# Delta-rule layers: v copied to SBUF by ScalarE, multiplied by beta on GpSimd, k and q projected to exchanged banks

## The chip, the cores and the metric

The kernel runs on one core of a Trainium2 chip. A core has five engines with queues of their own: TensorE (PE in the rows, PEld its weight loads), VectorE (DVE), ScalarE (ACT), GpSimd (POOL) and SyncE (SP), which only issues DMAs here. They work on SBUF, 128 partitions wide, and on PSUM, in which matmuls leave their results; GpSimd doesn't take part in reading PSUM here. Engines wait for each other through semaphores. The metric is the device time of one execution in microseconds, and lower is better.

## What is computed

Five stages in a row on x of 16 x 256 x 128: a convolutional token mixer, external attention with a Mamba layer, a mixture of experts, an attention block with two delta-rule ("fast weight") layers, and a second mixture of experts. The change touches the two delta-rule layers alone. The sequence is 254 long by then, there are 16 batches (B), 8 heads (H) and D = 64:

```python
def delta_rule(q, k, v, beta):
    def step(W, inp):
        qt, kt, vt, bt = inp
        wk = jnp.einsum('bhde,bhe->bhd', W, kt)
        v_new = bt * (vt - wk)
        W = W + jnp.einsum('bhd,bhe->bhde', v_new, kt)
        out = jnp.einsum('bhde,bhe->bhd', W, qt)
        return (W, out)
    ...
def fast_ff(x, ln_g, ln_b, slow_w, out_w):
    h = layer_norm(x, ln_g, ln_b)
    qkvb = jnp.einsum('sbi,oi->sbo', h, slow_w).reshape(slen, bsz, H, 3 * D + 1)
    q, k, v, beta = jnp.split(qkvb, [D, 2 * D, 3 * D], axis=-1)
    q = jax.nn.softmax(q, axis=-1)
    k = jax.nn.softmax(k, axis=-1)
    beta = jax.nn.sigmoid(beta)
    attn = delta_rule(q, k, v, beta)
    o = jnp.einsum('sbd,od->sbo', attn.reshape(slen, bsz, H * D), out_w)
    return x + o
```

## The kernel before

`fast_weights` (L1433) computes one such layer and is called twice. The recurrence over 254 tokens is cut into two chunks of 127 per batch, called lanes here (u = 0 and 1). Within a chunk it becomes a triangular system: A holds the products of beta*k with k, the inverse of its unit triangular form is applied to the right-hand side beta*v, and what comes out (`u_new`) gives the state and, with the masked products of q and k (`qk`), the outputs.

A pipeline of stages runs over the batches: `stage(b, ...)` prepares batch b, inverts batch b - 1 and substitutes batch b - 2. Stages 0 and 1 fill it (stage 0 only prepares, stage 1 prepares and inverts), 2 to 15 do all three, 16 and 17 drain it. Each engine walks through the same stages with an order of its own that is written out by hand; semaphores alone tie them. There is no scheduler.

What the engines do in a full stage:

- TensorE: projections of k, beta and q (`project`, L1658; `fw_w`, `fw_xs`), `below_blocks` and `corner_blocks` of the inverse (L1714, L1730), the turns of kb and k (`turn`, L1669), then for each lane the solves and joins (L1746, L1759, L1771), the sum A (`sum_a`, L1682), the projection of v, state, outputs (L1784, L1796, L1811, L1825, L1832), turns of q, the first qk sum (`sum_qk`, L1699), the output projection (L1841) and the second qk sum. Both qk sums of a lane go to two banks, one for even and one for odd heads.
- VectorE: per lane the maximum of k (L2002) and its shift (L2011), then `turn_blocks` (L2053), which turns the 32x32 blocks of the inverse of batch b - 1 that a DMA has brought to `fw_x_rows`; then beta, sums and reciprocals, maximum and shift of q; and between all that the inversion, `go_on` (L2075 product, L2079 subtraction), 31 such pairs in a row, each of which depends on the one before. In between stand `rest(0)` and `rest(1)` (L2044) and the `carried` subtraction (L2119). Behind the inversion come the two right-hand sides (L2037, from PSUM times beta), the mask of the first qk sum (L2059, even heads), the addition of the output projection (L2130) and the mask of the second.
- ScalarE: the exponentials, and nearly all copies out of PSUM, among them the odd heads of qk (L1914).
- GpSimd: kb and k (L1608, L1610), q (L1614), the copy of the next batch to `fw_xs` (L1617), the masks of the odd heads of qk (L1620) and the unit start of the next inversion (L1626).
- SyncE: when the last step of the inversion is done, it writes `fw_lane_x` to DRAM (L1568, two DMAs), reads the next A (L1573), reads the inverse back as rows (L1581, four DMAs, which the turn L2053 waits for) and to `fw_x_t` (L1585).

The banks of PSUM are shared between uses, and a use waits until the last one is read. k is projected to banks 4 and 5, where the qk sums of lane 1 lay, q to 7 and 3, where those of lane 0 lay. So the k projection of the next stage waits for the last mask of this one. The lane tiles of the inversion and `fw_rhs`, `fw_kb`, `fw_k_rows`, `fw_q_rows` are fp32 in SBUF.

## Time and profile before

| | before |
|---|---|
| time, median of 3 runs | 3078.03 us (3076.59 to 3078.49) |
| profiled execution | 3075.59 us, of which the trace spans 3073.7 us |
| VectorE busy | 2118.2 us, 69% |
| TensorE busy | 2422.8 us, 79% |
| ScalarE busy | 1209.8 us, 39% |
| GpSimd busy | 654.5 us, 21% |

The profile is of one execution. Busy shares are averages over stages with different limits, so a change in one layer is read from that layer: its stretch, its waits, and then one stage of it as a timeline. A wait is put down to what ended last by the trace. Spans on GpSimd are rough. The two layers lie at 1350 to 2016 us and at 2148 to 2811 us of the span.

### The profile page before, as it was taken

Reading aid. Unit: us, or ns where it says so; the run is one execution under the profiler, and the core shown is the slowest. Engines: PE = TensorE matmul, PEld = TensorE weight load, DVE = VectorE, ACT = ScalarE, POOL = GpSimd, SP = SyncE. Lnnn points to the kernel's source line nnn. Section 1 sums busy time; section 2 is a strip of 40 time slices with the busy share of each in tenths; the row PEclk is TensorE's granted clock in tenths of the full one; section 3 lists DMA queues with packets and bytes.
Section 4 is the critical chain, followed back from the end, with each engine's and each line's share of the span. In section 5 each row is a group of like instructions: output and inputs, shape, how many; then the busy total and the mean of one; then the engine's idle time right before and its main releaser. Section 6 shows DMA issues by size and latency. Waiting matters only on the chain. (4 is left out here: it accounts for less than half of the span.)

```text
span 3073.7 us, 43978 instructions
## 1 busy us (share of the span) xinstructions
PE 2422.8 (79%) x16426; PEld 1407.0 (46%) x16426; DVE 2118.2 (69%) x4507; ACT 1209.8 (39%) x1941; POOL 654.5 (21%) x632
## 2 busy tenths in 40 slices
PE   6757777777659999977888888777688888876598
PEld 2232222222234444335666666543466666665343
DVE  2347888888946777748888888612788888883332
ACT  4555444545423222243444444234343443441332
POOL 0004555555500000022222222101322222220000
PEclk9878888888879999988888988778798989986699
DMA  1000000000010000002222222210122222220000
GB/s 34 1 9 1 0 0 0 1 0 1 0 42 0 0 1 0 26 11 42 42 39 40 36 39 42 39 25 1 32 42 43 43 42 43 43 41 12 16 1 27
DMA packets 280817, 65.88 MB, mean 21 GB/s; under 512 B 272968, under 2 KB 274464, under 8 KB 280224
## 3 DMA queue, kind: packets, MB, share of 16 engines
q1 hardware_dynamic: 280608, 63.09, 11.0%
q8 instruction: 132, 2.16, 0.3%
q14 instruction: 77, 0.63, 0.1%
HBM read 44.20 MB, written 18.86 MB: 21 GB/s over the span
## 5 line engine op out<-in xcount | busy, mean ns | idle before, releaser
L907 POOL TENSOR_TENSOR ma_hc<-ma_state,ma_c 128x508 f32<-128x508 f32 x256 | 302.1, 1183 | 370.9 <-DVE ma_state L994 186.2
L2079 DVE TENSOR_TENSOR fw_lane_x<-fw_lane_x,fw_lane_p 128x126 f32<-128x126 f32 (+22 forms) x992 | 330.6, 333 | 34.0
L994 DVE TENSOR_TENSOR_SCAN ma_state<-ma_da,ma_ps_dbx 128x510 f32<-128x510 f32 x256 | 311.5, 1217 | 32.6 <-issue 24.1
L2075 DVE TENSOR_TENSOR fw_lane_p<-fw_lane_a,fw_lane_x 128x126 f32<-128x126 f32 (+22 forms) x992 | 273.5, 276 | 29.6
L1658 PE MATMUL fw_p<-fw_w,fw_xs 128*127 128x512 f32 (+1 forms) x512 | 238.2, 600 | 54.0 <-DVE fw_qk L2059 26.3
L809 PE MATMUL ma_ps_y<-ma_hc,const 128*128 128x508 f32 x480 | 257.1, 662 | 8.4 <-POOL ma_hc L907 8.4
L989 DVE TENSOR_TENSOR ma_ps_dbx<-ma_ps_b,ma_dtx 128x508 f32<-128x508 f32 x256 | 172.8, 675 | 39.6 <-PE ma_ps_b L793 39.1
L1094 ACT ACTIVATE ex_sig<-ex_gate,ex_gate_scaled 128x508 f32<-128x508 f32 x128 | 87.5, 683 | 271.2 <-PE ex_gate L1064 271.2
L886 ACT ACTIVATE ma_da<-ma_dt,ma_a 128x508 f32<-128x508 f32 x256 | 168.6, 708 | 39.3 <-DVE ma_dt L946 39.2
L793 PE MATMUL ma_ps_b<-ma_bc,select 128*128 128x508 bf16 x128 | 55.7, 435 | 146.5 <-DVE ma_ps_dbx L989 143.1
L1620 POOL TENSOR_TENSOR fw_qk<-fw_qk,fw_masks 128x512 f32<-128x512 f32 x64 | 82.4, 1289 | 403.2 <-ACT fw_qk L1914 403.2
L809 PEld LDWEIGHTS ma_ps_y<-ma_hc,const 128*128 128x128 f32 x480 | 102.7, 219 | 142.9 <-issue 89.2
L890 ACT ACTIVATE ma_c<-ma_ps_c 128x508 f32<-128x508 f32 x128 | 75.6, 591 | 230.6 <-PE ma_ps_c L796 225.9
L1658 PEld LDWEIGHTS fw_p<-fw_w,fw_xs 128*127 128x127 f32 x512 | 92.9, 218 | 132.3 <-issue 122.9
L1595 POOL MEMSET fw_k_rows<- 128x512 f32 x4 | 2.1, 524 | 660.7 <-POOLq L81 660.7
L1055 PE MATMUL ex_total<-ex_weighted,ex_down 128*128 128x508 f32 x256 | 130.8, 593 | 10.8 <-DVE ex_weighted L1119 10.8
L1108 DVE SCALAR_TENSOR_TENSOR ex_gelu<-ex_gate,ex_bias,ex_sig 128x508 f32<-128x508 f32 x128 | 95.6, 747 | 63.4 <-ACT ex_sig L1094 63.4
L1921 ACT ACTIVATE fw_u_new<-fw_p 64x512 f32<-64x512 f32 x128 | 75.7, 591 | 158.1 <-PE fw_p L1771 105.1
L1064 PE MATMUL ex_gate<-xn,ex_gate_up 128*128 128x508 f32 x256 | 131.7, 596 | 5.1 <-PEq L81 5.1
L1068 PE MATMUL ex_up<-xn,ex_gate_up 128*128 128x508 f32 x256 | 130.6, 592 | 0.0
L1614 POOL TENSOR_TENSOR fw_q_rows<-fw_q_rows,fw_total_q 127x512 f32<-127x512 f32 x64 | 66.7, 1042 | 286.3 <-DVE fw_total_q L2023 286.0
L1699 PE MATMUL fw_p<-fw_q_t,fw_k_t 64*128 64x128 f32 x1024 | 75.7, 288 | 64.4 <-issue 64.4
(304 smaller groups left out, 4898.4 us busy)
## 6 DMA issues: line engine op xcount, KB each, us to landing
fw_lane_a<-fw_a_dram SPq DMA_DIRECT2D x64, 256.0 KB, 4.1
fw_a_dram<-fw_a_t SPq DMA_DIRECT2D x128, 64.0 KB, 2.1
fw_x_dram<-fw_lane_x SPq DMA_DIRECT2D x64, 128.0 KB, 2.9
fw_x_rows<-fw_x_dram SPq DMA_DIRECT2D x128, 64.0 KB, 3.2
fw_x_t<-fw_x_dram SPq DMA_DIRECT2D x128, 64.0 KB, 2.7
x_in<-in_x SPq DMA_DIRECT2D x4, 512.0 KB
ex_gate_up<-in_gate_up SPq DMA_DIRECT2D x1, 2048.0 KB
out<-h SPq DMA_DIRECT2D x1, 2032.0 KB, 6.2
```

The lines of the kernel that those rows point to most:

```text
L809: pe.matmul(y_sum[h][:, 0:W2], k.ident, hc[(2 * n + h) % 8][:, :], start=n <= 1 and n - 1 in (-1, *PAIRED), stop=n == DS - 1)\
L886: act.activation(da[h][n % 4][:, :, 1:L + 1], two(dt[u][h][:, :]), ACT.Exp, scale=a[:, h, n:n + 1]).then_inc(s["da"], 1)
L907: pool.tensor_tensor(two(hc[m % 8][:, :]), state[m % 4][:, :, 1:L + 1], two(c_kept[n % 2][:, :]), ALU.mult).then_inc(s["hc"], 1)
L989: dve.tensor_tensor(dbx[h][:, :, 1:L + 1], two(b_all[:, 0:W2]), two(dtx[u][h][:, :]), ALU.mult).then_inc(s["dbx"], 1)
L994: dve.tensor_tensor_scan(line(state[m % 4][:, :, :]), line(da[h][n % 4][:, :, :]), line(dbx[h]), 0.0, ALU.mult, ALU.add).then_inc(s["scan" ...
L1055: pe.matmul(total[:, 0:W2], down[:, e, j, :], weighted[n % 2][:, :], start=False, stop=n == NHF - 1).then_inc(s["downed"], 1)
L1064: pe.matmul(gate[j][:, 0:W2], gate_up[:, e, j * H:(j + 1) * H], x, start=True, stop=True).then_inc(s["gated"], 1)
L1068: pe.matmul(up[j][:, 0:W2], gate_up[:, e, I0 + j * H:I0 + (j + 1) * H], x, start=True, stop=True).then_inc(s["upped"], 1)
L1108: dve.scalar_tensor_tensor(gelu[j][:, :], gate[j][:, 0:W2], bias[:, e, j:j + 1], sig[j][:, :], ALU.add, ALU.mult).then_inc(s["gelu"], 1)
L1658: pe.matmul(bank[0:C, bk, u * NH:u * NH + n] if name == "beta" else bank[0:C, bk, 0:n], xs[:, u * C:(u + 1) * C], w[:, at:at + n], start=T ...
L2075: dve.tensor_tensor(p, lane_a[:, j:j + 1, j + 1:BLOCK].to_broadcast(shape), lane_x[:, 0:shape[1], j:j + 1].to_broadcast(shape), ALU.mult)\
L2079: dve.tensor_tensor(below, below, p, ALU.subtract).then_inc(inverted[j], 1)
```

## The change

ScalarE copies the projected v of each lane from PSUM to a new SBUF tile, `v_rows`, and GpSimd multiplies it by beta into `rhs`; VectorE's `right_hand_side` is gone. k is projected to and turned from banks 7 and 3, q is projected to 4 and 5. The waits follow the banks: the k projection of a stage waits for the mask and the copy of the first qk sum, the second qk sum waits for the copies of v and no longer for `rhs`, and k of lane 1 is turned before kb of lane 1.

```diff
-        PROJ_K, PROJ_Q, PROJ_V, BETA = (4, 5), (7, 3), (4, 5), 6
-        TURN_K, TURN_KB, TURN_Q = (4, 5), (6, 7), (3, 6)
+        PROJ_K, PROJ_Q, PROJ_V, BETA = (7, 3), (4, 5), (4, 5), 6
+        TURN_K, TURN_KB, TURN_Q = (7, 3), (6, 7), (3, 6)
...
                 for u in chunks:
+                    pool.wait_ge(s["v"], c + u + 1)
+                    if substitutes:
+                        pool.wait_ge(s["second_sum"], c - 3 + u)
+                    pool.tensor_tensor(rhs[par][u][0:C], v_rows[u][:, :, :], wide(beta[:, u]), ALU.mult)\
+                        .then_inc(s["rhs"], 1)
+                for u in chunks:
                     pool.wait_ge(s["qk_copied"], c + u + 1)
...
                     if u == 0:
+                        pe.wait_ge(s["shift_q"], c + 2)
                         pe.wait_ge(s["k_t"], c + 2)
...
-                            pe.wait_ge(s["rhs"], c + 2)
+                            pe.wait_ge(s["v"], c + 2)
...
-                project("k", 0, PROJ_K[0], "qk_even", c)
-                project("k", 1, PROJ_K[1], "qk_copied", c)
+                project("k", 0, PROJ_K[0], "qk_even", max(c - 1, 0))
+                project("k", 1, PROJ_K[1], "qk_copied", max(c - 1, 0))
...
-                turn("kb", 1, kb[1], TURN_KB[1], "kb", "shift_q", c + 1)
                 turn("k", 1, k_rows[1], TURN_K[1], "rows_k", "shift_k", c + 2)
+                turn("kb", 1, kb[1], TURN_KB[1], "kb", "k_t", c + 1)
...
-                turn("q", 0, q_rows[0], TURN_Q[0], "rows_q", "shift_q", c + 2)
+                turn("q", 0, q_rows[0], TURN_Q[0], "rows_q", "k_t", c + 2)
...
+                def copy_v(u):
+                    if prepares:
+                        act.wait_ge(s["proj_v"], c + u + 1)
+                        act.wait_ge(s["rhs"], max(c + u - 1, 0))
+                        act.activation(v_rows[u][:, :, :], heads(bank[0:C, PROJ_V[u], :]), ACT.Copy)\
+                            .then_inc(s["v"], 1)
...
                     act.wait_ge(s["proj_beta"], c + 2)
+                    act.wait_ge(s["rhs"], c)
...
+                copy_v(0)
                 solved(1, 0)
                 copy_a(1)
+                copy_v(1)
                 turned("q", 0, TURN_Q[0], q_t[par][0])
...
-                def right_hand_side(u):
-                    if prepares:
-                        dve.wait_ge(s["proj_v"], c + u + 1)
-                        if substitutes:
-                            dve.wait_ge(s["second_sum"], upto[u])
-                        dve.tensor_tensor(rhs[par][u][0:C], heads(bank[0:C, PROJ_V[u], :]), wide(beta[:, u]), ALU.mult)\
-                            .then_inc(s["rhs"], 1)
...
                 go_on(20, BLOCK - 1)
-                right_hand_side(0)
-                right_hand_side(1)
                 mask_qk(0)
```

In a full stage the order on GpSimd is before (`fw_xs` is the next batch's input, `fw_qk` the products of q and k, `fw_lane_x` the inverse under work; the number behind a name is the lane):

```order
L1614 TENSOR_TENSOR fw_q_rows<-fw_q_rows,fw_total_q 127x512 x2
L1617 COPY fw_xs<-xn 128x254
L1620 TENSOR_TENSOR fw_qk_0<-fw_qk_0,fw_masks 128x512
L1620 TENSOR_TENSOR fw_qk_1<-fw_qk_1,fw_masks 128x512
L1626 COPY fw_lane_x<-fw_masks 128x512
```

and in the changed kernel:

```order
L1615 TENSOR_TENSOR fw_q_rows<-fw_q_rows,fw_total_q 127x512 x2
L1618 COPY fw_xs<-xn 128x254
L1623 TENSOR_TENSOR fw_rhs_0<-fw_v_rows,fw_beta 127x512
L1623 TENSOR_TENSOR fw_rhs_1<-fw_v_rows,fw_beta 127x512
L1627 TENSOR_TENSOR fw_qk_0<-fw_qk_0,fw_masks 128x512
L1627 TENSOR_TENSOR fw_qk_1<-fw_qk_1,fw_masks 128x512
L1633 COPY fw_lane_x<-fw_masks 128x512
```

Two products stand between the copy to `fw_xs` and the masks.

ScalarE in the middle of a full stage, before (`fw_k_first` keeps k of lane 0 for the state, `fw_u_new` is what a solve gives, `fw_a_t` is A, `fw_p` the PSUM banks):

```order
L1972 ACTIVATE fw_k_first<-fw_k_rows 127x512
L1921 ACTIVATE fw_u_new<-fw_p 64x512
L1907 ACTIVATE fw_a_t<-fw_p 128x1024
L1900 ACTIVATE fw_q_t_0<-fw_p 128x512
L1921 ACTIVATE fw_u_new<-fw_p 64x512
L1935 ACTIVATE fw_out_t<-fw_p 128x4x127
L1900 ACTIVATE fw_q_t_1<-fw_p 128x512
```

and in the changed kernel:

```order
L1988 ACTIVATE fw_k_first<-fw_k_rows 127x512
L1922 ACTIVATE fw_v_rows<-fw_p 127x512
L1936 ACTIVATE fw_u_new<-fw_p 64x512
L1915 ACTIVATE fw_a_t<-fw_p 128x1024
L1922 ACTIVATE fw_v_rows<-fw_p 127x512
L1908 ACTIVATE fw_q_t_0<-fw_p 128x512
L1936 ACTIVATE fw_u_new<-fw_p 64x512
L1950 ACTIVATE fw_out_t<-fw_p 128x4x127
L1908 ACTIVATE fw_q_t_1<-fw_p 128x512
```

One copy of v stands behind that of `fw_k_first`, the other behind the second of `fw_a_t`.

VectorE from the last step of an inversion to the turn of its blocks (`r` is the residual that the output projection is added to, `fw_top_k` the maxima of k), before:

```order
L2079 TENSOR_TENSOR fw_lane_x<-fw_lane_x,fw_lane_p 128x16
L2037 TENSOR_TENSOR fw_rhs_0<-fw_p,fw_beta 127x512
L2037 TENSOR_TENSOR fw_rhs_1<-fw_p,fw_beta 127x512
L2059 TENSOR_TENSOR fw_qk_0<-fw_p,fw_masks 128x512
L2130 TENSOR_TENSOR r<-fw_p,r 128x254
L2059 TENSOR_TENSOR fw_qk_1<-fw_p,fw_masks 128x512
L2002 TENSOR_REDUCE fw_top_k<-fw_p 127x8
L2011 TENSOR_TENSOR fw_k_rows<-fw_p,fw_top_k 127x512
L2002 TENSOR_REDUCE fw_top_k<-fw_p 127x8
L2011 TENSOR_TENSOR fw_k_rows<-fw_p,fw_top_k 127x512
L2053 STREAM_TRANSPOSE fw_x_turned<-fw_x_rows 128x512
```

and in the changed kernel:

```order
L2089 TENSOR_TENSOR fw_lane_x<-fw_lane_x,fw_lane_p 128x16
L2069 TENSOR_TENSOR fw_qk_0<-fw_p,fw_masks 128x512
L2138 TENSOR_TENSOR r<-fw_p,r 128x254
L2069 TENSOR_TENSOR fw_qk_1<-fw_p,fw_masks 128x512
L2020 TENSOR_REDUCE fw_top_k<-fw_p 127x8
L2029 TENSOR_TENSOR fw_k_rows<-fw_p,fw_top_k 127x512
L2020 TENSOR_REDUCE fw_top_k<-fw_p 127x8
L2029 TENSOR_TENSOR fw_k_rows<-fw_p,fw_top_k 127x512
L2063 STREAM_TRANSPOSE fw_x_turned<-fw_x_rows 128x512
```

The two right-hand sides are gone from between the inversion and the masks; nothing else in VectorE's order is moved.

## Rows read from the trace of the kernel before

**Rows 1.** Stretch, us; busy (x) of PE, PEld, DVE, ACT, POOL; PEclk; DMA share, GB/s.

```profile
1350.00:2016.00 666.00, 532.18 (x6478) 404.32 (x6479) 527.93 (x1452) 251.97 (x425) 157.19 (x162) 0.85 0.23 39
...
1614.88:1645.06 30.18, 26.69 (x391) 21.20 (x389) 27.72 (x83) 14.71 (x24) 7.99 (x8) 0.94 0.09 15
1645.06:1653.55 8.49, 6.20 (x28) 3.44 (x28) 5.58 (x9) 1.48 (x4) 1.82 (x2) 0.80 0.85 147
```

**Rows 2.** Waits of VectorE in layer 0 (total us, times, longest).

```profile
DVE fw_top_k L2002 <- PE fw_p L1658: 23.2, 16, 2.2
DVE fw_rhs L2044 <- PE fw_p L1759: 13.4, 12, 1.3
```

**Rows 3.** The same view of layer 1.

```profile
DVE fw_rhs L2044 <- PE fw_p L1759: 11.9, 10, 2.1
```

**Rows 4.** Timeline behind an inversion's end (start us, duration us, idle before in brackets).

```profile
1645.08 1.26 SPq L1568 DMA_DIRECT2D fw_x_dram<-fw_lane_x  x2
1645.09 1.29 DVE L2037 TENSOR_TENSOR fw_rhs<-fw_p,fw_beta 127x512 f32<-127x512 f32 x2
1646.29 0.68 DVE L2059 TENSOR_TENSOR fw_qk<-fw_p,fw_masks 128x512 f32<-128x512 f32 x1
...
1647.68 0.69 DVE L2059 TENSOR_TENSOR fw_qk<-fw_p,fw_masks 128x512 f32<-128x512 f32 x1 [0.37 <-PE fw_p L1699]
...
1648.65 1.90 SPq L1581 DMA_DIRECT2D fw_x_rows<-fw_x_dram  x4
...
1650.59 0.69 DVE L2002 TENSOR_REDUCE fw_top_k<-fw_p 127x8 f32<-127x512 f32 x1 [2.23 <-PE fw_p L1658]
...
1653.55 0.71 DVE L2053 STREAM_TRANSPOSE fw_x_turned<-fw_x_rows 128x512 f32<-128x512 f32 x1 [0.21 <-DMA fw_x_rows<-fw_x_dram]
```

**Rows 5.** Turned blocks in 14 stages; then the reads of one stage (ns min/median/max, first, last).

```profile
L2053 DVE STREAM_TRANSPOSE fw_x_turned<-fw_x_rows x14: 700/711/712, 1417.5 to 1930.1; 128x512 f32<-128x512 f32 x14
...
  DMA fw_x_rows<-fw_x_dram: 5.2, 8
...
L1581 SPq DMA_DIRECT2D fw_x_rows<-fw_x_dram x4: 308/488/953, 1610.2 to 1611.6; - x4
...
DMA to landing us min/median/max: 3.0/3.2/3.4
```

**Rows 6.** Groups by shape, VectorE, then GpSimd, in layer 0 (busy us, mean ns).

```profile
L2079 DVE TENSOR_TENSOR fw_lane_x<-fw_lane_x,fw_lane_p 128x16 f32<-128x16 f32 x14 | 16.1, 1147 | 0.5
L2079 DVE TENSOR_TENSOR fw_lane_x<-fw_lane_x,fw_lane_p 128x133 f32<-128x133 f32 x14 | 15.1, 1078 | 0.5
...
L2075 DVE TENSOR_TENSOR fw_lane_p<-fw_lane_a,fw_lane_x 128x133 f32<-128x133 f32 x14 | 3.4, 246 | 0.0
...
L2075 DVE TENSOR_TENSOR fw_lane_p<-fw_lane_a,fw_lane_x 128x16 f32<-128x16 f32 x14 | 2.7, 190 | 0.5
...
L1608 POOL TENSOR_TENSOR fw_kb<-fw_k_rows,fw_kb_scale 127x512 f32<-127x512 f32 x28 | 29.2, 1042 | 76.7 <-DVE fw_kb_scale L2029 76.7
```

**Rows 7.** Timeline: a GpSimd product and the VectorE instruction beside it.

```profile
1630.94 1.04 POOL L1614 TENSOR_TENSOR fw_q_rows<-fw_q_rows,fw_total_q 127x512 f32<-127x512 f32 x1 [4.87 <-DVE fw_total_q L2023]
1631.06 1.08 DVE L2079 TENSOR_TENSOR fw_lane_x<-fw_lane_x,fw_lane_p 128x133 f32<-128x133 f32 x1
```

**Rows 8.** Timeline: where the new work would stand.

```profile
1632.95 0.62 ACT L1972 ACTIVATE fw_k_first<-fw_k_rows 127x512 f32<-127x512 f32 x1
...
1637.03 1.02 ACT L1907 ACTIVATE fw_a_t<-fw_p 128x1024 f32<-128x1024 f32 x1 [1.63 <-PE fw_p L1759]
...
1638.69 1.15 PE L1771 MATMUL fw_p<-fw_rhs,fw_x_t 128*64 128x64 f32 x16
...
1642.90 1.99 PE L1841 MATMUL fw_p<-fw_out_t,fw_w_out 128*128 128x254 f32 x8
...
1643.69 1.32 POOL L1620 TENSOR_TENSOR fw_qk<-fw_qk,fw_masks 128x512 f32<-128x512 f32 x1 [9.72 <-ACT fw_qk L1914]
```

**Rows 9.** The view of rows 1 in a stretch of low clock.

```profile
1658.20:1665.00 6.80, 6.80 (x100) 6.24 (x100) 6.29 (x19) 3.59 (x6) 2.81 (x3) 0.50 0.00 0
```

More of the change, by code:

```diff
@@ L1480, in fast_weights @@
         q_rows = per("q_rows", [128, NH, D])
+        v_rows = per("v_rows", [C, NH, D])
         beta = sb("beta", [C, LANES, NH, 1])
@@ L1525, in fast_weights @@
             "exp_k", "exp_q", "total_k", "total_q", "recip_k", "recip_q", "rows_k", "rows_q",
-            "beta_exp", "beta_one", "beta", "kb", "rhs", "k_first", "turn_k", "turn_q", "turn_kb", "k_t", "q_t",
+            "beta_exp", "beta_one", "beta", "kb", "v", "rhs", "k_first", "turn_k", "turn_q", "turn_kb", "k_t", "q_t",
             "kb_t", "a_sum", "a_t", "qk_sum", "qk_even", "qk_copied", "qk_odd",
```

## The prediction, made before the changed kernel ran

> **What bounds the kernel now.** The change touches only the two delta-rule layers, so I read those. First the table by stretches [rows 1]: layer 0 takes 666 us (layer 1 much the same), and in it VectorE is busy 528 us. One stage of the loop then falls into two parts, and each has another limit. From the turn of the blocks (L2053) at 1614.88 to the end of the inversion at 1645.06, VectorE is busy 27.72 of 30.18 us, and much of the rest is the step between one lane instruction and the next: this part is bound by VectorE. From there to the next turn at 1653.55 it is busy 5.58 of 8.49 us, while the DMA engines are busy for 0.85 of the time.
>
> Next the waits of VectorE by what ended them [rows 2, 3]. In layer 0 it waits 23.2 us for the k projection, in 16 waits, and 13.4 us before `rest` (L2044) for TensorE, in 12; in layer 1 the latter is 11.9 us in 10. A reader who stops here expects a gain from both edits: two products fewer on VectorE, and a k projection that starts sooner. The timeline of the second part decides [rows 4]. Behind the inversion's end at 1645.06, VectorE does the two right-hand products (start 1645.09, the next instruction at 1646.29: 1.2 us for both), the masks and the addition until 1648.37, waits 2.23 us for k, works 2.8 us on the two maxima and shifts, and comes to L2053, where it waits 0.21 us more, for a DMA. Beside it runs another chain: L1568 writes the inverse at 1645.08, L1581 reads it back from 1648.65, and the last of those four reads lands just before 1653.55. So both chains are about 8.3 us long. In the turn's own view [rows 5] 8 of 14 turns wait for that DMA already; in the stage of 1614.88, where VectorE is last, the last read is issued at 1611.6 and lands 3.0 to 3.4 us later, at 1614.6 to 1614.9. The 14 turns span 1417.5 to 1930.1, 13 stages of 39.4 us. A stage is then: the VectorE part (about 31 us), and the DMA chain (about 8.2 us), which starts only when the inversion has ended.
>
> **What is taken from VectorE.** The two right-hand products leave its queue: 1.2 us per stage. The k projection no longer waits for the second qk mask (0.69 us) but for the first, and the second qk sum no longer waits for the right-hand sides, so most of the 2.23 us idle goes as well. After the change VectorE has behind the inversion: two masks and the addition, 1.8 us, a wait of some 1 us for k, and 2.8 us of maxima and shifts, 5 to 6 us in all. But the DMA chain stays at about 8.2 us, for nothing in it changes: it starts at the inversion's end, and SyncE's queue is the same. What is late next is the landing of L1581, at the same place. I book only what VectorE lies behind the landing now: nothing in the 8 turns that wait, some 0.1 to 0.3 us in most of the others, about 1 us in the first stage of a layer; by the turns one by one that is 3.8 us for both layers. **Term: -4 us** (bounds -3 and -5).
>
> **What is added to GpSimd.** 32 products a layer, v_rows by beta, 127x512 in fp32 from SBUF to SBUF. The same form is L1608: 1042 ns [rows 6]. GpSimd has room: it idles 9.72 us before its first qk mask [rows 8]. Its time is hidden, but it is not free for VectorE. The rows by shape show why [rows 6]: L2079 with 128x133 takes 1078 ns in all 14 stages, L2075 with the same shape 246 ns; with 128x16 it is 1147 against 190. The timeline shows what lies beside the long one [rows 7]: GpSimd's q product runs 1630.94 to 1631.98, and the VectorE instruction that starts at 1631.06 ends at 1632.14, just behind it. A lane product or subtraction, with two inputs in SBUF, doesn't get through while a GpSimd product runs, and the price is 1078 - 246 = 832 ns.
>
> Where do the new products land? v of lane 0 is projected early and its copy stands behind the k_first copy, which ends at 1633.57; so the copy (about 0.6 us) ends near 1634.2 and the product runs to 1635.2. v of lane 1 is copied behind a_t, from 1638.05 to about 1638.65, and its product also waits for `second_sum`, that is for L1771, which ends at 1639.84; it runs from 1639.9 to 1641 [rows 8]. Both stretches are nothing but lane instructions, and both are ahead of the inversion's end, in the part that VectorE bounds. Each costs 0.83 us or a little more; between that and the whole 1.04 I take 0.85, next to the row that shows the same case: 1.7 us per stage, for the 15 stages of a layer that prepare and invert: 30 x 1.7 = **+51 us**. From below the bound is one blocked instruction less a stage (+25), from above the whole 1042 ns each (+62).
>
> The Trainium skill, SBUF — State Buffer, under Practical consequences, says that a VectorE instruction with two SBUF inputs contends with a GpSimd instruction that reads SBUF, and that the later one fully blocks until the other is done. The trace agrees on who blocks, and prices it lower, at 0.83 us, because the instruction already under way goes on; by the page's whole instruction this term would be +62 us.
>
> **The ends of a layer.** In stage 0 nothing is inverted; the k projection of stage 1 starts one mask, 0.7 us, sooner: -1.5 us for both layers. In stage 1 nothing is substituted, so no output projection stands between the two qk sums; the second qk mask of GpSimd now falls into the inversion and costs 1147 - 190 = 0.96 us [rows 6], twice: +2 us.
>
> **What is moved or added at no cost.** ScalarE gets two copies of about 0.6 us a stage. Copy 0 stands before `solved(1,0)`, which waits for TensorE anyway; copy 1 stands behind a_t, where the copy of the turned q comes 0.6 us later, and its reader, the qk sum, stands behind three more groups of matmuls. If that cover were gone, the qk sums would come 0.6 us later, under an inversion that ends later still. k of lane 1 is turned before kb of lane 1: GpSimd writes kb first, so TensorE could start this pair up to 1 us later, but the corner blocks ahead of it in the queue take most of that time. `rest(1)` comes 0.85 us later (0.55 us of it was slack behind the q turn), hence L1771 and all behind it 0.3 us, under an inversion that is 1.7 us longer.
>
> **TensorE's clock.** The granted clock falls to 0.50, which is 1.2 GHz, for some time in the second part of the stage (0.80 on average over its 8.49 us [rows 1]) and again from 1658.2 to 1665 [rows 9]; this later stretch lies on the way to `rest(0)`. That waits for TensorE 1.1 us (13.4 / 12) where it waits, in 22 of 28 stages, and (13.4 + 11.9) / 28 = 0.9 us over all [rows 2, 3]. After the change TensorE has no work for about 3 us between the projections and the turn, where now one follows close on the other. I expect the clock to fall sooner, around the turn, and the corner blocks and turns of the next stage to start up to 0.9 us later. Nothing shows how soon it rises again. Bounds: the wait goes altogether (28 x -0.9 = -25 us), or each is 2.1 us (28 x +1.2 = +34 us). I take 0.5 us a stage, between the ends and nearer to no change: **+14 us**.
>
> **Sum.** 51 - 4 - 1.5 + 2 + 14 = +61.5 us. Against the profiled execution's 3075.6 us that is 3137; against the median of 3078.0, which is 2.4 us above it, 3139.5. I forecast **3139 us**, 2% slower.
>
> **Rivals.**
> A, *the clock helps*: TensorE no longer idles before the second qk sum and the k projection, the low stretch goes, and with it the wait of `rest(0)`. For: one of the two low stretches of this stage lies there. Against: the new idle stretch at the turn. 3078 + 47.5 - 25 = 3100 us. Chance 0.15.
> B, *the second qk mask too*: the second qk sum now follows the output projection at once, and GpSimd's second mask would start near 1647.1 (the projection ends 0.3 us later than now, at 1645.2 [rows 8]; then the sum, 1.2 us, and the copy, 0.6), only 0.3 us behind the new inversion's end (1646.75). If it starts before the last lane instruction in every stage, 28 x 0.96 = +27 us: 3166 us. It decides at 0.3 us. Chance 0.10.
> C, *no blocking*: the new products fall beside instructions that VectorE runs with an input in PSUM, or beside waits, and the ends of the two parts stay where they are. Then the terms of 51, 2 and 14 us go: 3078 - 5.5 = 3072 us. It would take that none of the two lands beside a lane instruction; but from 1633.4 to 1645 there is one other, L2044. Chance 0.04.
> D, *the saving counts*: the landing follows VectorE, so that the second part shrinks by the 2.5 us that it has less. 3078 + 47.5 - 75 = 3050 us. It needs a landing within 6 us of the inversion's end; the rows show about 8. The Trainium skill, Perfetto Trace Analysis, under Optimizing Scalar/DVE Operations, holds that with VectorE saturated, moving work to ScalarE or even GpSimd may make sense, and adds that the shared read port may spoil it; by the first half D, by the second the forecast. Chance 0.03.
>
> **Chances.** Forecast 0.68, A 0.15, B 0.10, C 0.04, D 0.03. The range from 3100 to 3166 takes in A, B and the bounds of the clock. A measurement of this kernel can tell about 0.2% (6 us). Slower 0.93, same 0.03 (most of C), faster 0.04 (D and the rest of C).
>
> **What the profile after would show.** Right: two lane instructions more per stage, of 1.05 to 1.1 us, in the groups by shape; the turn in all stages waiting for the DMA, 2 to 3 us each, about 75 us in all; from turn to turn about 41.5 us; the wait for k halved. The forecast is wrong in its main term if those lane instructions keep their 0.3 us, in the second if the time from L1568 to the turn falls well under 8 us, and in the clock term if L2044 waits much less than 25 us in all, or more than 60 us.

## The result, and the profile after

The changed kernel takes 3126.48 us (median of 4 runs, 3124.32 to 3128.36), the kernel before 3077.31 us beside it (4 runs). The ratio is 1.0162, with a 95% interval of 1.015 to 1.0175: 1.6% slower, +49 us. The traces span 3122.7 and 3073.7 us, which is +49.0 us too. The prediction said 3139, between 3100 and 3166. Of the executions of the kernel before that the experiments are compared with, one took 3595.4 us at a granted clock of 0.63; it stands in no ratio.

First the two parts of one stage, the stretches that answer to [rows 1] (stretch, its length, then busy time of PE, PEld, DVE, ACT, POOL, granted clock, DMA share, GB/s):

```profile
1624.73:1657.61 32.88, 29.33 (x404) 24.15 (x404) 29.32 (x82) 15.26 (x26) 10.11 (x10) 0.84 0.08 12
1657.61:1666.24 8.63, 4.11 (x12) 1.87 (x12) 4.29 (x7) 1.72 (x4) 1.88 (x2) 0.99 0.82 141
```

The part that VectorE bounds, from the turn to the inversion's end, took 30.18 us in the stage shown before and 32.88 in this one. The part behind it lasts 8.63 us against 8.49, though VectorE is busy for 4.29 us of it only, where it was 5.58. What was taken from VectorE is gone from the second part and has shortened nothing.

Over the 28 full stages, two by two from trace to trace, the first part takes 915.6 us in sum and took 870.9 (+44.7), the second 232.0 and took 231.8 (+0.2).

The groups by shape, VectorE in layer 0, the view of [rows 6]:

```profile
L2085 DVE TENSOR_TENSOR fw_lane_p<-fw_lane_a,fw_lane_x 128x128 f32<-128x128 f32 x14 | 16.4, 1169 | 0.5
L2085 DVE TENSOR_TENSOR fw_lane_p<-fw_lane_a,fw_lane_x 128x45 f32<-128x45 f32 x14 | 16.2, 1155 | 0.5
...
L2089 DVE TENSOR_TENSOR fw_lane_x<-fw_lane_x,fw_lane_p 128x108 f32<-128x108 f32 x14 | 13.9, 991 | 0.5
...
L2089 DVE TENSOR_TENSOR fw_lane_x<-fw_lane_x,fw_lane_p 128x128 f32<-128x128 f32 x14 | 4.1, 291 | 0.5
...
L2085 DVE TENSOR_TENSOR fw_lane_p<-fw_lane_a,fw_lane_x 128x108 f32<-128x108 f32 x14 | 3.8, 273 | 0.5
...
L2089 DVE TENSOR_TENSOR fw_lane_x<-fw_lane_x,fw_lane_p 128x16 f32<-128x16 f32 x14 | 2.6, 187 | 0.5
```

Two long lane instructions have come in, 128x128 (1169 ns against 291 for the same shape, +0.88 us) and 128x108 (991 against 273, +0.72 us), in all 14 stages. The one beside GpSimd's first qk mask is still there, but is another one: 128x45 now, since the inversion ends later, and 128x16 takes 187 ns where it took 1147. The timeline shows the two products with what stands beside them:

```profile
1644.43 0.59 ACT L1922 ACTIVATE fw_v_rows<-fw_p 127x512 f32<-127x512 f32 x1
...
1645.10 1.04 POOL L1623 TENSOR_TENSOR fw_rhs<-fw_v_rows,fw_beta 127x512 f32<-127x512 f32 x1 [0.17 <-ACT fw_v_rows L1922]
1645.12 1.17 DVE L2085 TENSOR_TENSOR fw_lane_p<-fw_lane_a,fw_lane_x 128x128 f32<-128x128 f32 x1
...
1650.09 1.12 PE L1779 MATMUL fw_p<-fw_rhs,fw_x_t 128*64 128x64 f32 x16 [0.37 <-DVE fw_rhs L2054]
...
1651.35 1.05 POOL L1623 TENSOR_TENSOR fw_rhs<-fw_v_rows,fw_beta 127x512 f32<-127x512 f32 x1 [5.21 <-PE fw_p L1779]
1651.54 0.99 DVE L2089 TENSOR_TENSOR fw_lane_x<-fw_lane_x,fw_lane_p 128x108 f32<-128x108 f32 x1
```

The first product starts with the end of the v copy at 1645.1, and the lane instruction of 1645.12 ends at 1646.29, behind the product's 1646.14. The second waits for the second solve (L1779), as forecast, and starts while another lane instruction is under way; the next one starts 0.19 us behind it, so it loses 0.72 us and not 0.88. Together 1.60 us a stage.

The second part of the same stage, which answers to [rows 4]:

```profile
1657.64 1.26 SPq L1569 DMA_DIRECT2D fw_x_dram<-fw_lane_x  x2
1657.64 0.69 DVE L2069 TENSOR_TENSOR fw_qk<-fw_p,fw_masks 128x512 f32<-128x512 f32 x1
...
1658.58 0.68 DVE L2069 TENSOR_TENSOR fw_qk<-fw_p,fw_masks 128x512 f32<-128x512 f32 x1
...
1659.61 0.69 DVE L2020 TENSOR_REDUCE fw_top_k<-fw_p 127x8 f32<-127x512 f32 x1 [0.35 <-PE fw_p L1665]
...
1661.19 1.90 SPq L1582 DMA_DIRECT2D fw_x_rows<-fw_x_dram  x4
```

VectorE goes from the inversion straight to the masks, waits 0.35 us for k where it waited 2.23, and is done with the last shift near 1662.3. The DMA chain is what it was: written at 1657.64, read back from 1661.19. The waits of VectorE in layer 0 (total, times, longest), against [rows 2]:

```profile
DVE fw_x_turned L2063 <- DMA fw_x_rows<-fw_x_dram: 54.2, 15, 6.5
DVE fw_rhs L2054 <- PE fw_p L1767: 14.4, 14, 1.2
DVE fw_top_k L2020 <- PE fw_p L1665: 4.6, 13, 0.4
```

The wait for k fell from 23.2 to 4.6 us, and the turn waits for its DMA in every stage. Without the last turn of the layer (6.5 us) it is 47.7 us in 14 turns, where the kernel before had 8 such waits, 5.2 us together, in as many [rows 5].

### The profile page after: what moved, and what is told of

Its sections match the earlier page's. It is cut to its first block and busy times, and to the rows that moved or that the text cites. A ratio compares the mean times of both kernels' runs of the same rounds, so it can differ in the third digit from the quotient of the medians.

```text
span 3122.7 us, 44170 instructions
## 1 busy us (share of the span) xinstructions
PE 2432.2 (78%) x16426; PEld 1428.0 (46%) x16426; DVE 2126.3 (68%) x4443; ACT 1240.8 (40%) x2005; POOL 723.7 (23%) x696
## 5 line engine op out<-in xcount | busy, mean ns | idle before, releaser
L2085 DVE TENSOR_TENSOR fw_lane_p<-fw_lane_a,fw_lane_x 128x126 f32<-128x126 f32 (+22 forms) x992 | 325.5, 328 | 29.6
L1665 PE MATMUL fw_p<-fw_w,fw_xs 128*127 128x512 f32 (+1 forms) x512 | 217.5, 556 | 77.9 <-DVE fw_qk L2069 50.2
L1722 PE MATMUL fw_p<-fw_x_turned,fw_a_t 32*32 32x32 f32 x2048 | 59.9, 233 | 141.2 <-issue 141.2
L1665 PEld LDWEIGHTS fw_p<-fw_w,fw_xs 128*127 128x127 f32 x512 | 84.8, 201 | 144.3 <-issue 134.6
L1722 PEld LDWEIGHTS fw_p<-fw_x_turned,fw_a_t 32*32 32x32 f32 x2048 | 56.6, 148 | 164.6 <-issue 164.6
```

What stands on the lines that cost most here:

```text
L1665: pe.matmul(bank[0:C, bk, u * NH:u * NH + n] if name == "beta" else bank[0:C, bk, 0:n], xs[:, u * C:(u + 1) * C], w[:, at:at + n], start=T ...
L1722: mm = pe.matmul(bank[rows_of(g + 1), BELOW, n * BLOCK:(n + 1) * BLOCK], a_t[par][rows_of(g), u, r, p, rows_of(g + 1)], x_turned[rows_of(g ...
L2085: dve.tensor_tensor(p, lane_a[:, j:j + 1, j + 1:BLOCK].to_broadcast(shape), lane_x[:, 0:shape[1], j:j + 1].to_broadcast(shape), ALU.mult)\
```

## The experiments

All are compared with the kernel before on the same chip (3073.8 us for the first four, 3076.9 for the next, 3076.4 for the last), and a time below is a median.

### GpSimd's products taken away, and moved

**VectorE makes the products**, from the copies in SBUF; the rest of the change stays.

```diff
-                for u in chunks:
-                    pool.wait_ge(s["v"], c + u + 1)
-                    ...
-                    pool.tensor_tensor(rhs[par][u][0:C], v_rows[u][:, :, :], wide(beta[:, u]), ALU.mult)
...
                 go_on(20, BLOCK - 1)
+                right_hand_side(0)
+                right_hand_side(1)
```

> The changed kernel with one edit: the two products v_rows by beta are made by VectorE behind the inversion, as the right-hand sides were before, and not by GpSimd. The copies by ScalarE and the exchanged banks stay. Theory (GpSimd's products hold up the lane instructions): both stalls, 1.60 us a stage and 2.5 us in stage 1 of a layer, go, and the products are hidden under the DMA chain that ends at the turn; the time is 3126 - 28 x 1.6 - 5 = 3076 us, that is 3070 to 3079, the same as the kernel before or up to 0.2% faster. Rival (the copies on ScalarE or the exchanged banks cost the time): stays within 5 us of 3126.

3083.5 us, ratio 1.0035 (1.0021 to 1.0049). That is 9.7 us more than the kernel before, where the changed one takes 49.2 more: 40 of the 49 us are gone, so the products on GpSimd are the cost. But it is 4.5 us above the upper end of what was expected. The waits say why (layer 0):

```profile
DVE fw_x_turned L2065 <- DMA fw_x_rows<-fw_x_dram: 29.3, 13, 2.7
DVE fw_rhs L2056 <- PE fw_p L1761: 19.4, 14, 2.1
```

The wait of `rest(0)` is 19.4 us in this layer, 39.0 us over the 28 full stages, where it was 25.5 in the kernel before. With that taken off, the first part of the stages is what it was, but for 2 us (882.4 - 39.0 against 870.9 - 25.5). The stalls beside new products are gone, and 13.5 us of TensorE's lateness have come.

**The products behind the masks**, still on GpSimd:

```diff
-                for u in chunks:
-                    pool.wait_ge(s["v"], c + u + 1)
-                    ...
                 for u in chunks:
                     pool.wait_ge(s["qk_copied"], c + u + 1)
                     ...
+                for u in chunks:
+                    pool.wait_ge(s["v"], c + u + 1)
+                    ...
```

> The changed kernel with one edit: GpSimd makes the same two products behind its two qk masks, not ahead of them. Theory: they then fall behind the inversion's end, where VectorE reads PSUM or waits for the DMA, and hold nobody up: the long lane instructions beside them are gone, the time is 3070 to 3080 us. If the second mask, which stands ahead of them, moves into the inversion instead, up to 28 x 0.95 = 27 us more. Rival (GpSimd's added work costs by its amount, wherever it stands): 3126.

3086.9 us, 1.005 (1.0031 to 1.0069). It is the same amount of work on GpSimd as in the changed kernel, and 36 of the 49 us are gone (13.1 us over the kernel before). The two shapes that were long are short again:

```profile
L2089 DVE TENSOR_TENSOR fw_lane_x<-fw_lane_x,fw_lane_p 128x128 f32<-128x128 f32 x14 | 4.1, 292 | 0.5
...
L2089 DVE TENSOR_TENSOR fw_lane_x<-fw_lane_x,fw_lane_p 128x108 f32<-128x108 f32 x14 | 3.8, 272 | 0.5
```

The place of the products counts, not their amount. Beside them VectorE now runs the shifts of k, whose large input lies in PSUM; these take 692 ns with a product beside them and 691 without. Here too `rest(0)` waits longer, 37.1 us over the full stages, 11.6 us more than before, and the time stands 7 us above what was expected.

### The products alone

```diff
                 for u in chunks:
+                    if substitutes and u == 1:
+                        pool.wait_ge(s["second_sum"], c - 2)
+                    pool.tensor_tensor(spare[u][0:C, 0:NH], spare[u][0:C, NH:2 * NH],
+                                       wide(spare[u][0:C, NH:2 * NH, 0:1]), ALU.mult)
+                for u in chunks:
                     pool.wait_ge(s["qk_copied"], c + u + 1)
```

> The kernel before with one addition: GpSimd makes two products of 127x512 from SBUF to spare tiles, at the place where the change puts its own (the second also behind the second solve). Nothing else of the change. Theory: the price alone, 28 x 1.6 + 2 x 1.7 = 48 us or so: 3118 to 3130 us. Rival (the price of the change comes from the copies of v, the banks or the new waits): 3077 us, as before.

3127.9 us, 1.0182 (1.0165 to 1.0199): the kernel before with nothing but two idle products is 54 us slower, where the change made it 49. The time is made up otherwise, though. The stalls are in the first part (898.4 us, +27.5; the wait of `rest(0)` has given back 13.3 there), and the second part grew by 19.2 us, for here VectorE still has its long chain behind the inversion and waits more in it (layer 0, against 23.2 and 5.2 us before):

```profile
DVE fw_top_k L2008 <- PE fw_p L1664: 33.8, 25, 2.2
DVE fw_qk L2065 <- PE fw_p L1705: 11.3, 13, 1.3
```

The granted clock is low in other places of the stage: for 3.9 of the first 13 us behind a turn on average, against 6.0. So the near equality of this run and the change is in part chance. What the products alone do to the lane instructions can be read from their lengths: they are held up for 1.43 us more a stage, 40 us over the full stages (1.60 and 45 in the changed kernel, where the first product starts at another moment of a lane instruction). The rest of the 54 us are waits that moved.

**Memsets in their place**, which only write:

```diff
-                    pool.tensor_tensor(spare[u][0:C, 0:NH], ...)
+                    pool.memset(spare[u][:, :, :], 0.0)
```

> As the run with two spare products, but with memsets of 128x1024 in place of the products, which take about as long and only write to SBUF. If what VectorE and GpSimd exclude each other from is the reading of SBUF, the lane instructions keep their 0.3 us, and the time is that of before, 3074 to 3081 us. If any work of GpSimd in SBUF holds them up, it is 3118 to 3130 us like the products. The Trainium skill, SBUF - State Buffer, Practical consequences, says the former: a GpSimd instruction that only writes does not contend with one of two SBUF inputs.

3079.2 us, 1.0017 (1.0008 to 1.0027), as the first of the two cases expected. GpSimd is nearly as long at work there (949 ns each), and the lane instructions do not notice. First GpSimd's group:

```profile
L1622 POOL MEMSET fw_spare<- 128x1024 f32 x28 | 26.6, 949 | 70.5 <-PE fw_p L1776 70.5
```

VectorE by shape:

```profile
L2080 DVE TENSOR_TENSOR fw_lane_p<-fw_lane_a,fw_lane_x 128x128 f32<-128x128 f32 x14 | 4.1, 292 | 0.5
...
L2084 DVE TENSOR_TENSOR fw_lane_x<-fw_lane_x,fw_lane_p 128x108 f32<-128x108 f32 x14 | 3.8, 272 | 0.5
```

It is the reading of SBUF by GpSimd that holds up a VectorE instruction with two inputs there, as the Trainium skill, SBUF — State Buffer, Practical consequences, says; these rows agree.

### The DMA chain behind the inversion

SyncE's read of the next A goes behind the reads of the inverse:

```diff
-                if prepares:
-                    sp.wait_ge(s["a_out"], a_written)
-                    ...lane_a...
                 if inverts:
                     ...x_rows..., ...x_t...
+                if prepares:
+                    sp.wait_ge(s["a_out"], a_written)
+                    ...lane_a...
```

In the changed kernel:

> The changed kernel with one edit in SyncE's order: the read of the next A (fw_lane_a) is issued behind the reads of the inverse (fw_x_rows, fw_x_t), not ahead of them. Theory: the DMA chain from the inversion's end to the turn bounds the second part of each stage; in the last stages of a layer, where no A is read, it takes 7.1 us and not 8.2, so it becomes about 7.1 us everywhere and the time falls by 28 x 1.1 = 31 us to about 3095 (3088 to 3105). Rival (VectorE's own work or TensorE bounds this part): 3126, no change.

In the kernel before:

> The same order of SyncE in the kernel before. Theory: there VectorE's own chain behind the inversion is as long (8.0 to 8.3 us with its waits), so the shorter DMA chain brings only what VectorE waits for the DMA now, some 12 us in all, and less where the clock of TensorE turns against it: 3062 to 3074 against 3074. Rival (the DMA chain alone bounds both kernels): 31 us less here too, 3043.

3116.4 us (1.0128, 1.0109 to 1.0146) and 3058.6 us (0.9938, 0.9917 to 0.9959). Both expectations missed. The second part did shrink in the changed kernel, from 232.0 to 206.8 us over 28 stages (7.4 us each): the DMA chain bounds it, as the theory has it. But the first part grew from 915.6 to 937.2, by 21.6 us. The wait of `rest(0)` went from 26.8 to 47.9 us; VectorE also waits 6 us for the next A, which comes later now, but these waits cost nothing on balance: the first lane instruction (128x31), which comes later by them, is held up by GpSimd's product beside it for 7 us less. What is left is the wait of `rest(0)`. Layer 0:

```profile
DVE fw_x_turned L2063 <- DMA fw_x_rows<-fw_x_dram: 35.3, 13, 4.0
DVE fw_rhs L2054 <- PE fw_p L1767: 24.7, 14, 2.0
...
DVE fw_lane_p L2085 <- DMA fw_lane_a<-fw_a_dram: 3.3, 7, 0.7
```

In the kernel before, the second part shrank from 231.8 to 219.7 us only, since VectorE's own chain is nearly as long there; the first grew by 4.5. That is 8 us of the 15 that the spans show (3058.6 against 3073.7); the rest lies between the layers, from the last turn of one layer to the first of the next (207.0 and then 198.4 us). The one inversion in there is followed by a second part as long as before (9.4 us), so the edit brought nothing in it, and the cause of the 8.6 us stays open. So the comparison stands on the parts of the stages, not on the total.

### The clock of TensorE

Four runs bear on the term for the clock. **The exchanged banks alone**, on the kernel before:

```diff
-        PROJ_K, PROJ_Q, PROJ_V, BETA = (4, 5), (7, 3), (4, 5), 6
-        TURN_K, TURN_KB, TURN_Q = (4, 5), (6, 7), (3, 6)
+        PROJ_K, PROJ_Q, PROJ_V, BETA = (7, 3), (4, 5), (4, 5), 6
+        TURN_K, TURN_KB, TURN_Q = (7, 3), (6, 7), (3, 6)
```

with the waits and the turns' order of the change, but for those that speak of v.

> The kernel before with the exchanged banks and their waits alone: VectorE still makes both right-hand sides from PSUM behind the inversion, ScalarE copies no v, GpSimd has nothing new. Theory: the k projection starts earlier, VectorE's chain behind the inversion falls below the DMA chain (about 7.1 against 8.2 us), the gain is 4 to 5 us and is more than taken back by the clock, which falls sooner because TensorE is idle ahead of the turn; like the run with VectorE's product from SBUF, 3078 to 3086 against 3074. If instead the two copies on ScalarE made that run slower, this one is 3066 to 3072.

3088.4 us, 1.0038 (1.0027 to 1.0049). The run with the copies of v on ScalarE had 1.0035; the copies cost nothing that can be measured, and the exchange of banks costs 12 us, 2 more than the upper end of what was expected. The second part, which was to shrink by 4 to 5 us, takes 234.8 us, +3.0: VectorE now waits for the landing of the reads in every stage, but they land later, at 8.36 us behind the inversion's end against 8.20. The first part of the full stages takes 884.3 us, +13.4, and `rest(0)` waits 40.7 us, +15.2. In one stage, with its turn at 1615.2 (busy time and, third from last, the granted clock):

```profile
1612.20:1615.20 3.00, 1.11 (x3) 0.19 (x1) 0.83 (x2) 0.91 (x3) 0.00 (x0) 1.00 1.06 134
1615.20:1619.20 4.00, 2.03 (x68) 1.83 (x68) 3.79 (x10) 1.81 (x3) 2.02 (x2) 0.77 0.15 23
...
1622.20:1626.20 4.00, 4.00 (x30) 3.52 (x27) 3.66 (x13) 2.46 (x5) 0.81 (x1) 0.50 0.00 0
1626.20:1629.20 3.00, 2.79 (x32) 2.53 (x32) 1.04 (x4) 0.64 (x2) 0.23 (x1) 0.77 0.00 0
```

TensorE is busy for 1.11 us of the three ahead of the turn, then the clock goes to 0.50 and is there until 11 us behind the turn and more (0.77 in the last stretch).

**Filler ahead of the turn**: two matmuls into a free bank, in the changed kernel.

```diff
+                    pe.wait_ge(s["out_t"], outputs_before)
+                    if prepares:
+                        for _ in range(2):
+                            pe.matmul(bank[0:C, BELOW, :], xs[:, 0:C], w[:, 0:512], start=True, stop=True)
                     settle()
                     pe.wait_ge(s["x_turned"], batches)
-                    pe.wait_ge(s["out_t"], outputs_before)
```

> The changed kernel with one addition: in each full stage TensorE makes two matmuls of 127x512 into a bank that is free, between the q projection and the wait for the turned blocks; nobody reads them. Theory: the granted clock falls because TensorE is idle some 3 us there; with the idle time filled the low stretch behind the turn shortens, and rest(0), which waits 27 us in all, waits less: 3100 to 3118. Rival (the low stretch has another cause, or the wait of rest(0) does not hang on the clock): 3126, or more, if the filler itself delays the blocks.

3125.7 us, 1.0153 (1.0134 to 1.0171): nothing, as the rival has it. First the changed kernel, in the 3 us ahead of a turn, then from 0 to 4, 4 to 7 and 7 to 11 us behind it:

```profile
1621.70:1624.70 3.00, 0.00 (x0) 0.00 (x0) 0.00 (x0) 0.36 (x1) 0.00 (x0) 1.00 1.21 145
1624.70:1628.70 4.00, 2.76 (x68) 2.53 (x68) 3.80 (x10) 1.18 (x2) 2.03 (x2) 0.56 0.18 24
1628.70:1631.70 3.00, 3.00 (x70) 2.50 (x68) 2.76 (x8) 1.82 (x3) 2.06 (x3) 0.50 0.03 5
1631.70:1635.70 4.00, 4.00 (x30) 3.55 (x28) 3.66 (x13) 2.49 (x5) 0.81 (x1) 0.54 0.00 0
```

and the run with the filler, from 0 to 4, 4 to 7 and 7 to 11 us behind its turn at 1624.3:

```profile
1624.30:1628.30 4.00, 2.02 (x68) 1.58 (x68) 3.82 (x10) 1.81 (x3) 2.04 (x2) 0.93 0.10 12
1628.30:1631.30 3.00, 2.86 (x68) 2.50 (x68) 2.76 (x8) 1.20 (x2) 2.04 (x2) 0.50 0.03 5
1631.30:1635.30 4.00, 4.00 (x34) 3.60 (x32) 3.66 (x13) 2.71 (x5) 0.83 (x1) 0.59 0.00 0
```

The filler did what it was to do: the clock is 0.93 and not 0.56 in the first 4 us, and over the 28 stages it is low for 7.1 of the first 13 us and not for 9.9. But it is low from then on and recovers at the same place (10.3 us behind the turn on average in both), and `rest(0)` waits 26.8 us, as in the changed kernel. Not the length of the low stretch sets that wait but its end, since the solve and join ahead of `rest(0)` lie there.

**Filler behind the below blocks**, again in the changed kernel:

```diff
                     mm.then_inc(s["below_sum"], 1)
+                    if prepares:
+                        pe.wait_ge(s["added"], batches_before)
+                        pe.matmul(bank[0:C, CORNER, :], xs[:, 0:C], w[:, 0:512], start=True, stop=True)
```

> The changed kernel with one addition: one matmul of 127x512 into a free bank behind the below blocks, where TensorE waits for kb. The wait of rest(0) went with the end of the low stretch, not with its beginning: filler ahead of the turn took 3.4 us off its beginning and nothing off the wait. Theory A: TensorE's clock stays low because too little runs on the full array behind the turn, and the filler ends the low stretch earlier: the wait of rest(0) falls from 0.96 us a stage to below 0.5, 3105 to 3118. Theory B: the end doesn't move, and the filler, which takes 1.2 us at the high and over 2 us at the low clock, holds the turns of kb and k: the wait grows by 0.3 to 1 us a stage, 3130 to 3152.

3110.0 us, 1.0111 (1.0092 to 1.013), 16 us less than the changed kernel. The same stretches of a stage with its turn at 1621.6:

```profile
1621.60:1625.60 4.00, 3.16 (x66) 2.54 (x67) 3.80 (x10) 1.18 (x2) 2.03 (x2) 0.50 0.14 18
1625.60:1628.60 3.00, 3.00 (x36) 2.12 (x35) 2.76 (x8) 1.72 (x3) 2.05 (x3) 0.53 0.02 5
1628.60:1632.60 4.00, 3.99 (x90) 3.56 (x84) 3.66 (x13) 3.08 (x6) 0.82 (x1) 1.00 0.00 0
```

Now the clock is back at 1.00 by 7 us behind the turn (by 7.8 us in 24 of the 28 stages; in the other four it comes back at 10.5 to 11.4 us, and in three of them `rest(0)` waits 2.0 us), and `rest(0)` waits 11.6 us in all. That is 15.2 us less, and the first part of the full stages takes 15.7 us less. Work that nobody uses, on the path and 1.1 to 2.1 us long, makes the kernel faster. That is the outcome of theory A: with the filler the low stretch ends sooner. The reason that A gives for it is not shown by that. Without it TensorE, busy with the 32x32 blocks and the turns for 2.76 of the first 4 us and all of the next 7, stays at the low clock. Which property of the added matmul brings the clock back, no run shows.

**The rests two lane steps later**, in the changed kernel:

```diff
-                go_on(6, 8)
+                go_on(6, 10)
                 rest(0)
-                go_on(8, 12)
+                go_on(10, 12)
                 sums("q", 1)
                 inverse_sums("q", 1)
-                go_on(12, 14)
+                go_on(12, 16)
                 ...
-                go_on(14, 20)
+                go_on(16, 22)
                 rest(1)
-                go_on(20, BLOCK - 1)
+                go_on(22, BLOCK - 1)
```

> The changed kernel with one edit in VectorE's order: rest(0), the carried subtraction and rest(1) each stand two lane steps (four instructions, about 1.2 us) later, so that VectorE has lane work where it waits for TensorE now. Theory: the wait of rest(0), 26.9 us in all, is a real part of the time and goes nearly whole: 3126 - 20 to 27 = 3099 to 3106. Rival: TensorE's own chain from the solve to the carried subtraction is as tight, and the wait only moves there: 3120 to 3127.

3111.5 us, 1.0111 (1.0092 to 1.0129). That is 15 us less than the changed kernel, not 20 to 27. The wait fell from 26.8 to 15.5 us only: the low stretch ends 1.7 us later behind the turn than in the changed kernel (12.0 against 10.3 on average). The part of the wait that went was real time; the rest moved with the clock.

### What the parts make together

The products behind the masks, both masks held until the inversion has ended, A read behind the inverse, two filler matmuls ahead of the turn:

```diff
+                if inverts:
+                    pool.wait_ge(inverted[-1], b)
                 for u in chunks:
                     pool.wait_ge(s["qk_copied"], c + u + 1)
                     ...
+                for u in chunks:
+                    pool.wait_ge(s["v"], c + u + 1)
+                    ...
```

> The changed kernel with four edits: GpSimd's products stand behind the qk masks; both masks wait for the last step of the inversion; A is read behind the inverse; two filler matmuls as in the run with those alone. Theory, from 3087 for the products behind the masks (against 3074 for the kernel before): the stall beside the first mask goes (28 x 0.95 = 27 us), the DMA chain is 1.1 us shorter (31 us), and up to 25 us of the wait of rest(0): 3005 to 3030, clearly below both kernels. Rival: once VectorE's stalls and the chain are shorter, its own work behind the inversion (5 to 6 us) or GpSimd's (5 us, then unit start and kb) is late, and half of the sum is lost: 3040 to 3060.

3028.8 us, 0.9842 (0.9825 to 0.986), within what was expected. The holding of the masks was not run alone. And the same without the filler and with the rests later:

> The run with all four edits, without the filler matmuls, and with the rests two lane steps later. Theory: 3029 less the wait of rest(0), which is 31 us there: 3000 to 3010. If the filler did something after all, its lack costs some of that: up to 3020.

3008.8 us, 0.9779 (0.9762 to 0.9797), also within what was expected: 2.2% faster than the kernel before. The last lane steps are short now (128x16: 189 ns against 1147 [rows 6]), the first part takes 827.5 us against 870.9 over 28 stages, the second 211.8 against 231.8. With the stalls gone VectorE waits for others (layer 0):

```profile
DVE r L2140 <- PE fw_p L1851: 17.0, 14, 1.2
DVE fw_x_turned L2065 <- DMA fw_x_rows<-fw_x_dram: 15.7, 15, 3.6
DVE fw_qk L2071 <- PE fw_p L1709: 9.5, 14, 0.7
```

`r` is the addition of the output projection, now the longest of its waits. It costs nothing yet: it lies ahead of the turn, and the turn still waits for its DMA in all 28 stages, 24.8 us together. In half of them that is 0.6 us or less, so the DMA chain still ends the second part, and TensorE's chain to `r` is close behind it.

## Why the prediction was right, and where it was off

By its own terms, with what the traces show:

| term | forecast | measured |
|---|---|---|
| lane instructions held up by the products | +51 (25 to 62) | +47.9 |
| second qk mask falls into the inversion of stage 1 | +2 | +2.0 |
| stage 0 ends sooner | -1.5 | -1.4 |
| what VectorE lay behind the landing | -4 (-5 to -3) | -1.8 |
| `rest(0)` and the clock | +14 (-25 to +34) | +1.3 |
| sum | +61.5 | +48.0 |

The measured sum leaves 1.0 us of the 49.0 between the spans. Outside these terms there are small differences of either sign, for which no run gives a cause: layer 0 starts 1.15 us later, layer 1 as much sooner behind the last turn of layer 0, the last stages of the layers take 1.1 us more in sum, what follows layer 1 takes 1.2 us more, and one wait of 1.2 us ahead of the `carried` subtraction is gone.

**The stalls.** Right in kind, place and price: 28 x (0.88 + 0.72) = 44.8, and 1.57 in each of the two stages that invert but do not yet substitute. The second product costs less than the 0.85 assumed because it starts while a lane instruction is under way. That the products cost by their place and not by their amount is shown by moving them (36 of the 49 us gone), and the price of a place beside lane instructions by adding idle ones.

**The removal.** Right: the two right-hand sides lay under the DMA chain, and it is still 8.26 us from the inversion's end to the landing on average (8.20 before). VectorE has even less to do ahead of it than forecast: 4.7 us in the stage shown, and not 5 to 6, since k comes 0.35 us late and not 1 us. So the turn waits longer, 97.2 us in the 28 turns that were to wait about 75. The -4 became -1.8: the first stages gave 2.0 us, as expected, but the 1.7 us or so in the full stages went to reads that landed later, 231.4 against 229.7 us in sum.

**The clock, mis-sized.** The step "the clock falls sooner and the blocks and turns start later" holds: in the changed kernel it is low for 9.9 of the first 13 us behind a turn on average, and was for 6.0. The step from there to the wait of `rest(0)`, 0.5 us more a stage, does not; it measured 0.05: the wait depends on where the low stretch ends, and this moves with the kernel. In the changed kernel it ends near 10.3 us behind each turn and `rest(0)` waits 0.96 us; with VectorE's products it often ends at 12 and more, and the wait is 1.39; with A read last 1.71. So the term, as forecast, is there when the banks alone are exchanged (+15.2 us of wait), and by the changed kernel's own timing it is nearly gone. The range allowed for that; the value could not be chosen from the trace before, and that the total still came within 13 us of the forecast rests on the first term, of which the runs above show the cause.

**The rivals.** A (the clock helps) fails: the low stretch grew. B fails, by as little as forecast: GpSimd's second mask starts at 1658.07 in the stage shown, 0.46 us behind the inversion's end at 1657.61. C and D fail with the rows of the result: the lane instructions are held up, and the second part keeps its length.

## What to carry to other kernels

An instruction taken from the busiest engine brings nothing where another chain of the same length runs beside it; look at each part of a stage for what ends it, and shorten that chain first. Work given to GpSimd that reads SBUF held up the VectorE instructions with two inputs in SBUF that came beside it here (fp32), and not those with their large input in PSUM: hold it back until the latter are up. Where such a part hangs on TensorE, look at the granted clock around it, and at work that can be put ahead of the wait.

## What the runs showed of the hardware that was not expected

- A matmul that nobody needs, 1.1 to 2.1 us long and on the path, made the kernel 16 us faster, by bringing the granted clock from 0.50 back to 1.00 some 3 us sooner in most stages (low for 6.1 of the first 13 us behind a turn, and not for 9.9). Two of them in an idle stretch just ahead of the turn changed where the clock fell and gained nothing.
- Every edit of the timing moved the low stretches of the clock against the stage, and with them the wait of `rest(0)`, between 6 and 48 us in all. Differences of 10 to 20 us between variants of this kernel can be that alone, and only the parts of the stages tell.
- The read of the next A, 256 KB per DMA, between the write and the read back of the inverse makes the latter 0.9 us later; issued behind them it is late itself, and VectorE's first lane step waits for it in 7 of the 14 stages of layer 0, 0.5 us each. That instruction is held up less by GpSimd then, so the late read cost nothing on balance.
